# An interaction tower on one core: products read from PSUM instead of from copies, new orders and banks, earlier ids, layer-1 weights in five pieces

## The chip, the cores and the metric

One core of a Trainium2 chip runs the whole kernel. The metric is device time in microseconds of one execution. TensorE (PE in the rows) multiplies matrices, VectorE (DVE), ScalarE (ACT) and GpSimd (POOL) work on elements, SyncE (SP) issues transfers. Matmuls write only PSUM, which has eight banks of 512 fp32 columns on 128 partitions.

## The reference, cut to what matters

```python
e = jnp.stack([tbl_f[ids[:, f]] for f in range(40)], axis=1)   # 512 x 40 x 32
vi, vj = e[:, I, :], e[:, J, :]                                # the 780 pairs i < j
z = jnp.einsum('bke,kef,bkf->bk', vi, W, vj)                   # 512 x 780
h = jnp.concatenate([z, dense_ctx], axis=1)                    # 512 x 796
h = jnp.maximum(h @ W_top1 + b_top1, 0.0)                      # 512
h = jnp.maximum(h @ W_top2 + b_top2, 0.0)                      # 256
y = h @ W_top3
```

## The kernel before, in words

**Quads.** The 40 fields are packed four by four into 10 quads; `emb[:, q, :]` holds quad q as 4 x 32 partitions by 512 batch columns. Quads 0, 1, 3 and 5 are "hot" (tables of 1000 or 1250 rows) and are looked up on TensorE: `spread` (L541) copies the ids to all partitions, ScalarE turns them to fp16 (`ids_to_16`), VectorE (26 of them, L480) or ScalarE (10 of them, two passes, L399 and L402) makes a one-hot tile for each 128 table rows, and `look_up` (L554) multiplies it with the table, split into three bf16 pieces (`rest_of_first`, `third_piece` on VectorE). Quads 2, 4, 6, 7, 8 and 9 are gathered: GpSimd issues 96 indirect DMAs (L375), 16 for each quad in this order, each of 128 rows; `turn` (L572) waits for a quad's 16 and transposes it. ScalarE copies ("lands", L409 and L412) each quad from PSUM into `emb`.

**Pairs.** Group g is one of the 55 pairs (slots quad, stream quad). `map_group` (L584) multiplies the stream quad by the packed pair weights; this fills two operations' worth of PSUM (one where both quads are the same), each a pair of banks, 128 x 1024. There are 100 operations o = 0 to 99. A weight step (`multiply`, L311) multiplies an operation's two banks by `emb` of the slots quad into `prod`, a ring of 8. `sum_ops(b)` (L600) adds over the 32 dimensions of operations 2b and 2b+1 on TensorE into `z_ps`; ScalarE saves it to `zt` after each 8 sums. `layer1` (L617) is the first layer in three parts of z tiles (0, 1), (2, 3), (4), four column blocks m each, and a tail (5, 6). The tail, the second layer (L659) and the output (L665) end the program.

**Who multiplies.** VectorE does 93 operations: 73 read `ring_ps` in PSUM, 20 (COPIED_OPS) read a copy in SBUF, `copied`, that ScalarE makes (L423). GpSimd cannot read PSUM; it does 7 (POOL_OPS) from such copies, behind its 96 gathers.

**Orders and banks.** Each engine's order is written out by hand as a string of letters, and each engine runs it strictly in order. TensorE: i spread, l look-up tile, t turn, m map, s sum, 1 layer 1. VectorE: r pieces, o one-hot, w weight, a layer-1 add. ScalarE: I ids, o one-hot, L land, c copy, z save, 1 layer-1 save. `BANKS` gives the PSUM banks of each step, and `banks_free` (L525) makes TensorE wait until the last user of a bank is done: the weight step of the operation, or only its copy where there is one. Below, M22 is the map of group 22, s16 the sum of operations 32 and 33, w32 the weight step of operation 32, c71 the copy of operation 71, H2.3 tile 3 of hot quad number 2, T6 the turn of quad 6, L1.0 layer 1 of part 1 and block 0.

**Transfers.** ScalarE's queue issues the ids of the hot fields and then those of the gather (`idx`). SP issues tables and pair weights from the start, and the weights of both layers (1792 and 512 KB, L363 and L364) once all look-ups are done; every layer-1 step waits for both.

Of the kernel before, what the change touches and what calls it, by code (L numbers as in the profile page):

```python
# [26 lines left out]
P = 128  # L27
BATCH = 512
CHUNKS = BATCH // P
FIELDS = 40  # L30
DIM = 32
SLOTS = P // DIM
# [18 lines left out]
def quads():  # L51
# [3 lines left out]
    for vocab in HOT_VOCABS:  # L55
# [35 lines left out]
RING_TABLE = 3  # L91
RING_HOT = 2
RING_COPY = 4

PARTS = [(0, 1), (2, 3), (4,)]
TAIL = (5, 6)

TENSOR_ORDER = ("iillllllilllilllllmllmmtlllmlsllslmlllmmssmsmmstslmlllmlslmlllmmlsmssmssmstmsmsmm1mssmssm1mstmmsmssm"  # L100
                "1msmsm1mstmsmmssmssm1mssm1mssm1mtmmssmssm1mssmssms1m11msssmm1s")


BANKS = ("0240624304042065202024024024660240240240240206420242064024026403042402460242026406204024020640241422"
         "4642604204246024024604320402462301")

VECTOR_ORDER = ("rooooorooooooooooroowwwwooowworwwwwwwwwwooowwwowowwwwwwwwwwwwwwwwwwwwwwwwwwwwwwwwwwwwwwwwwwwwwwwwwww"
                "wwwawwwwaawwwwwawwwwwwwaawawwwa")


SCALAR_ORDER = ("IIoIIIIILIoLoLooLooLooozLcccLzc1cLcc1zc1c1ccLcczcccccLcccczcccczc")

POOL_OPS = [77, 78, 80, 85, 87, 93, 98]
COPIED_OPS = [28, 32, 34, 37, 45, 47, 48, 54, 56, 60, 62, 64, 67, 69, 73, 75, 81, 84, 89, 92]
SCALAR_ONE_HOTS = [4, 17, 21, 23, 25, 27, 30, 31, 34, 35]


def z_place(t):
# [64 lines left out]
def build(nc, ctx_rows, ids, hot_ids, tables, hot_tables, w_pairs, consts, vocab_rows, w1, w2, out):  # L183
    with ExitStack() as ctx:
# [6 lines left out]
        def sem(name):  # L191
            return ctx.enter_context(nc.semaphore(name))
# [42 lines left out]
        vocab_loaded = sem("vocab_loaded")  # L235
        const_loaded = sem("const_loaded")
        ctx_loaded = sem("ctx_loaded")
        mlp_loaded = sem("mlp_loaded")
        wload = [sem(f"wload{q}") for q in range(QUADS)]
        gathered = [sem(f"gathered{k}") for k in range(len(GATHERED_AT))]  # L240
        hot_ids_loaded = sem("hot_ids_loaded")
# [95 lines left out]
        @block.sync  # L337
        def _(sp):
            def load_table(h):
                if h >= RING_TABLE:  # L340
                    sp.wait_ge(one_hot_used, FIRST_ONE_HOT[h - RING_TABLE + 1])
                sp.dma_start(table[:, h % RING_TABLE, :width(h)], hot_tables[h]).then_inc(table_loaded[h], 16)

            def load_weights(q):
                first = GROUPS.index((0, q))
                sp.dma_start(wall[:, first:first + q + 1, :].rearrange("p g n -> p (g n)"),
                             w_pairs[:, first * P:(first + q + 1) * P]).then_inc(wload[q], 16)

            load_table(0)
            sp.dma_start(vocab[:], vocab_rows).then_inc(vocab_loaded, 16)  # L350
            load_table(1)
            load_weights(0)
            load_weights(1)
            sp.dma_start(consts_sb[:], consts).then_inc(const_loaded, 16)
            load_weights(2)
            load_table(2)
            for q in range(3, QUADS):
                load_weights(q)
            for h in range(RING_TABLE, len(HOT_AT)):
                load_table(h)  # L360
            sp.dma_start(ctx_sb[:], ctx_rows).then_inc(ctx_loaded, 16)
            sp.wait_ge(one_hot_used, FIRST_ONE_HOT[-1])
            sp.dma_start(w1_sb[:], w1.rearrange("k p n -> p k n")).then_inc(mlp_loaded, 16)  # L363
            sp.dma_start(w2_sb[:], w2.rearrange("(k p) n -> p k n", p=P)).then_inc(mlp_loaded, 16)  # L364
            sp.wait_ge(y_saved, 1)
            sp.dma_start(out.rearrange("(c b) o -> c (b o)", b=P), y_sb[::DIM, :]).then_inc(stored, 16)
            sp.wait_ge(stored, 16)
# [16 lines left out]
        def _(act):  # L384
# [49 lines left out]
                                     bias=b1_sb[:, m:m + 1]).then_inc(lin_saved, 1)  # L434

            act.dma_start(ids_sb[:], hot_ids).then_inc(hot_ids_loaded, 16)  # L436
            act.dma_start(idx[:].rearrange("p c f -> p (c f)"), ids).then_inc(ids_loaded, 16)
            act.wait_ge(hot_ids_loaded, 16)
            nc.scalar.activation(ids_rows[:], ids_sb[:], ACT.Copy).then_inc(ids_rows_done, 1)  # L439
            for kind, what in ACT_STEPS:  # L440
# [83 lines left out]
        def _(pe):  # L524
# [100 lines left out]
            for kind, what in PE_STEPS:  # L625
                if kind == "spread":
                    spread(what)
                elif kind == "hot":
                    look_up(*what)
                elif kind == "turn":  # L630
                    turn(what)
                elif kind == "map":
                    map_group(what)
                elif kind == "sum":
                    sum_ops(what)
                else:
                    part, m = what
                    pe.wait_ge(z_saved, PARTS[part][-1] + 1)
                    pe.wait_ge(mlp_loaded, 32)
                    banks_free(("layer1", what))  # L640
                    layer1(bank(("layer1", what)), PARTS[part], m).then_inc(lin_done, 1)

            pe.wait_ge(z_saved, TAIL[0] + 1)
            for m in range(M1):
                banks_free(("tail", m))
                layer1(bank(("tail", m)), TAIL[:1], m, stop=False)
                if m == 0:
                    sum_ops(LAST // 2)
# [4 lines left out]
            for m in range(M2):  # L653
                for k in range(M1):
                    if m == 0:
                        pe.wait_ge(h1_ready, k + 1)
                    for c in range(COLUMNS):
                        first = m * P + DIM * c
                        mm = nc.tensor.matmul(h2_ps[m][DIM * c:DIM * (c + 1), :], w2_sb[:, k, first:first + DIM],  # L659
# [90 lines left out]
```

## Time and profile before

| | us |
|---|---|
| median of 3 runs | 190.03 |
| lowest and highest | 189.29, 190.49 |
| the profiled execution | 191.81 |
| its span, first to last instruction | 190.0 |

The page gives busy time of each engine. TensorE is busy for 92% of the span, VectorE 78%, GpSimd 61%, ScalarE 48%. "PE L595" and the like in a row name engine and line of the kernel; "idle before" is time in which the engine sat still ahead of an instruction, with what ended it. A matmul in fp32 has two records, so a map of a full group is a row of x16, a sum or one layer-1 step over one z tile x8.

### The profile page before, as it was taken

Reading aid. Unit: us, or ns where it says so; the run is one execution under the profiler, and the core shown is the slowest. Engines: PE = TensorE matmul, PEld = TensorE weight load, DVE = VectorE, ACT = ScalarE, POOL = GpSimd, SP = SyncE. Lnnn points to the kernel's source line nnn. Section 1 sums busy time; section 2 is a strip of 40 time slices with the busy share of each in tenths; the row PEclk is TensorE's granted clock in tenths of the full one; section 3 lists DMA queues with packets and bytes.
Section 4 is the critical chain, followed back from the end, with each engine's and each line's share of the span. In section 5 each row is a group of like instructions: output and inputs, shape, how many; then the busy total and the mean of one; then the engine's idle time right before and its main releaser. Section 6 shows DMA issues by size and latency. Waiting matters only on the chain.

```text
span 190.0 us, 4602 instructions
## 1 busy us (share of the span) xinstructions
PE 174.8 (92%) x1976; PEld 47.3 (25%) x1976; DVE 148.2 (78%) x141; ACT 92.0 (48%) x83; POOL 115.8 (61%) x107
## 2 busy tenths in 40 slices
PE   1999949998999996999999999999999799999993
PEld 0243303321233222122122112222222122222331
DVE  0999987999999786598899898897975868882500
ACT  4877995989699520261072335252255332230421
POOL 0777777877877777778777777877068180522000
PEclk9999999999999999699999999999999999999999
DMA  5999310100000194000111000000000000000000
GB/s 187 388 410 337 106 17 10 19 10 17 16 14 16 39 352 147 17 10 10 17 14 17 11 14 16 13 14 14 3 3 0 0 3 3 0 0 3 0 3 0
DMA packets 7164, 10.80 MB, mean 57 GB/s; under 512 B 2004, under 2 KB 4696, under 8 KB 7144
## 3 DMA queue, kind: packets, MB, share of 16 engines
q1 hardware_dynamic: 3896, 8.81, 12.6%
q0 software_dynamic: 3072, 1.58, 4.8%
q8 instruction: 16, 0.26, 0.6%
q10 hardware_dynamic: 176, 0.12, 0.3%
q14 instruction: 4, 0.03, 0.0%
HBM read 10.50 MB, written 0.00 MB: 55 GB/s over the span
## 4 chain that ended last, share of the span: by engine, by line
PE 55%; POOL 26%; issue 8%; DMA 6%; DVE 2%; ACT 2%; ACTq 0%; DVEq 0%
POOL rows L375 26%; PE ring_ps L595 21%; PE z_ps L612 16%; PE ring_ps L621 13%; PE ring_ps L659 4%; DMA rows<-table,idx 4%; DMA idx<-ids 2%; DVE prod L314 2%; ACT copied L423 1%; PE ring_ps L580 1%; ACT h L458 0%; ACT emb L412 0%; PE ring_ps L665 0%; ACTq L436 0%; DVE y_sb L521 0%
## 5 line engine op out<-in xcount | busy, mean ns | idle before, releaser
L375 POOL DMA_INDIRECT rows<-table,idx x96 | 99.0, 1031 | 33.7 <-issue 28.9
L314 DVE TENSOR_TENSOR prod<-ring_ps,emb 128x1024 f32<-128x1024 f32 x73 | 86.8, 1220 | 16.4 <-PE ring_ps L595 15.6
L595 PE MATMUL ring_ps<-emb,wall 32*64 32x512 f32 (+1 forms) x800 | 61.2, 620 | 3.6 <-DVE prod L314 2.3
L423 ACT ACTIVATE copied<-ring_ps 128x1024 f32<-128x1024 f32 x27 | 27.6, 1025 | 57.7 <-PE ring_ps L595 54.8
L612 PE MATMUL z_ps<-prod,consts_sb 128*32 128x512 f32 x400 | 50.7, 609 | 0.1
L314 DVE TENSOR_TENSOR prod<-copied,emb 128x1024 f32<-128x1024 f32 x20 | 26.6, 1333 | 5.0 <-ACT copied L423 5.0
L314 POOL TENSOR_TENSOR prod<-copied,emb 128x1024 f32<-128x1024 f32 x7 | 16.6, 2377 | 22.5 <-ACT copied L423 22.5
L621 PE MATMUL ring_ps<-zt,w_sb 128*32 128x512 f32 x224 | 26.7, 597 | 0.0
L595 PEld LDWEIGHTS ring_ps<-emb,wall 32*64 32x64 f32 (+1 forms) x800 | 12.9, 131 | 44.3 <-issue 21.1
L399 ACT ACTIVATE distance<-ids,vocab 128x2048 f16<-128x2048 f16 x10 | 20.0, 2000 | 1.7 <-PE ring_ps L567 1.2
L402 ACT ACTIVATE one_hot<-distance,vocab 128x2048 bf16<-128x2048 f16 x10 | 20.0, 2002 | 0.3
L612 PEld LDWEIGHTS z_ps<-prod,consts_sb 128*32 128x32 f32 x400 | 9.9, 109 | 34.9 <-issue 20.6
L480 DVE TENSOR_SCALAR one_hot<-ids,vocab 128x2048 bf16<-128x2048 f16 x26 | 17.9, 746 | 0.4 <-ACT ids L387 0.4
L567 PE MATMUL ring_ps<-one_hot,table 128*32 128x512 bf16 x144 | 14.9, 402 | 0.0
L567 PE MATMUL ring_ps<-one_hot,rest 128*32 128x512 bf16 x144 | 14.6, 394 | 0.0
L567 PE MATMUL ring_ps<-one_hot,third 128*32 128x512 bf16 x144 | 14.6, 393 | 0.0
L621 PEld LDWEIGHTS ring_ps<-zt,w_sb 128*32 128x32 f32 x224 | 6.6, 109 | 18.5 <-issue 16.1
L549 PE MATMUL ring_ps<-ids_rows 16*128 16x512 f16 x16 | 5.8, 500 | 4.5 <-ACT ids_rows L439 4.3
L387 ACT ACTIVATE ids<-ring_ps 128x1024 f16<-128x1024 f32 x8 | 7.8, 1019 | 3.4 <-PE ring_ps L549 3.4
L466 DVE TENSOR_TENSOR rest<-table 128x1024 f32<-128x1024 f32 (+1 forms) x4 | 5.4, 1348 | 4.5 <-DMA table<-hot_table 4.5
L580 PE MATMUL ring_ps<-consts_sb,rows 128*128 128x128 f32 x24 | 3.8, 283 | 4.0 <-DMA rows<-table,idx 3.9
L427 ACT ACTIVATE zt<-z_ps 128x512 f32<-128x512 f32 x6 | 3.6, 595 | 7.5 <-PE z_ps L612 7.5
(25 smaller groups left out, 56.4 us busy)
## 6 DMA issues: line engine op xcount, KB each, us to landing
w_sb<-w SPq DMA_DIRECT2D x1, 1792.0 KB, 8.0
rows<-table,idx POOLq DMA_INDIRECT x96, 2.4
table<-hot_table SPq DMA_DIRECT2D x2, 640.0 KB, 5.5
table<-hot_table SPq DMA_DIRECT2D x2, 512.0 KB, 4.1
wall<-w_pairs SPq DMA_DIRECT2D x1, 640.0 KB
wall<-w_pairs SPq DMA_DIRECT2D x1, 576.0 KB, 9.1
wall<-w_pairs SPq DMA_DIRECT2D x1, 512.0 KB, 8.1
w_sb<-w SPq DMA_DIRECT2D x1, 512.0 KB, 9.8
```

Source lines behind the costliest of these rows:

```text
L314: return eng.tensor_tensor(prod[:, o % RING_P], products, emb[:, slots:slots + 1, :].to_broadcast([P, 2, BATCH]), ALU.mult)
L375: nc.gpsimd.indirect_dma_start(rows[:, k, c, r, :], None, tables[f], bass.IndirectOffsetOnAxis(ap=idx[:, c, f:f + 1], axis=0)).then_inc(ga ...
L387: nc.scalar.activation(ids16[:, h, 2 * half:2 * half + 2, :], pair(("spread", h), half), ACT.Copy).then_inc(ids16_done, 1)
L399: nc.scalar.activation(distance[:], ids16[:, h].rearrange("p r b -> p (r b)"), ACT.Abs, bias=vocab_column(h, t, -1)).then_inc(distance_don ...
L402: nc.scalar.activation(one_hot[:, n % RING_ONE_HOT, :], distance[:], ACT.Relu, bias=vocab[:, 4 * MAX_TILES:], scale=-1.0).then_inc(one_hot ...
L423: nc.scalar.activation(copied_op(o), op_banks(o), ACT.Copy).then_inc(copied_ready, 1)
L480: nc.vector.tensor_scalar(one_hot[:, n % RING_ONE_HOT, :], ids16[:, h].rearrange("p r b -> p (r b)"), vocab_column(h, t), None, ALU.is_equ ...
L567: mm = nc.tensor.matmul(bank(("hot", (h, 0)))[DIM * r:DIM * (r + 1), :], shaped[:, r, t, :], one_hot[:, n % RING_ONE_HOT, r * BATCH:(r + 1 ...
L595: mm = nc.tensor.matmul(pair(("map", g), i // 2)[half, i % 2, :], wall[own, g, half], emb[own, stream, :], start=True, stop=True)
L612: mm = nc.tensor.matmul(z_ps[DIM * g:DIM * (g + 1), :], sel[:, m, :], prod[:, t // 2 % RING_P, t % 2, :], start=m == 0, stop=last)
L621: mm = nc.tensor.matmul(bank[DIM * c:DIM * (c + 1), :], w1_sb[:, k, first:first + DIM], zt[:, k, :], start=start and k == ks[0], stop=stop ...
L659: mm = nc.tensor.matmul(h2_ps[m][DIM * c:DIM * (c + 1), :], w2_sb[:, k, first:first + DIM], h1[:, k, :], start=k == 0, stop=k == M1 - 1)
```

## The change

VectorE takes no operation from a copy any more: COPIED_OPS is empty, so 92 weight steps of VectorE read PSUM, and ScalarE copies only for GpSimd, which has 8 operations (71, 79, 83, 84, 86, 87, 90, 92) in place of 7 (77, 78, 80, 85, 87, 93, 98). The strings of all three orders and of the banks are new. The gather's ids are issued by SP ahead of everything else, in place of second on ScalarE's queue. The layer-1 weights come in four pieces, one for each part, and the second layer's as a fifth; SP issues them after the last look-up and after the third gathered quad has come (`gathered[2]`, quad 6), and each layer-1 part waits for its own piece only.

```diff
--- before.py
+++ after.py
@@ -91,28 +91,29 @@
 RING_TABLE = 3
 RING_HOT = 2
 RING_COPY = 4
+W1_BEHIND = 2
 
 PARTS = [(0, 1), (2, 3), (4,)]
 TAIL = (5, 6)
 
 
 
-TENSOR_ORDER = ("iillllllilllilllllmllmmtlllmlsllslmlllmmssmsmmstslmlllmlslmlllmmlsmssmssmstmsmsmm1mssmssm1mstmmsmssm"
-                "1msmsm1mstmsmmssmssm1mssm1mssm1mtmmssmssm1mssmssms1m11msssmm1s")
-
-
-BANKS = ("0240624304042065202024024024660240240240240206420242064024026403042402460242026406204024020640241422"
-         "4642604204246024024604320402462301")
-
-VECTOR_ORDER = ("rooooorooooooooooroowwwwooowworwwwwwwwwwooowwwowowwwwwwwwwwwwwwwwwwwwwwwwwwwwwwwwwwwwwwwwwwwwwwwwwww"
-                "wwwawwwwaawwwwwawwwwwwwaawawwwa")
-
-
-SCALAR_ORDER = ("IIoIIIIILIoLoLooLooLooozLcccLzc1cLcc1zc1c1ccLcczcccccLcccczcccczc")
-
-POOL_OPS = [77, 78, 80, 85, 87, 93, 98]
-COPIED_OPS = [28, 32, 34, 37, 45, 47, 48, 54, 56, 60, 62, 64, 67, 69, 73, 75, 81, 84, 89, 92]
-SCALAR_ONE_HOTS = [4, 17, 21, 23, 25, 27, 30, 31, 34, 35]
+TENSOR_ORDER = ("iiillllllllillllmlllltlmllmlmllmllslsmlsmsmtllllmsmlmslmlsmslmmllsmsmsmssmstmssmm1mssm1mssmtsmmssmsm"
+                "1msm1mssmssmtmsmssm1mssmtsm1mssm1mmsmssm1msm1sms1m1sm1smssmsms")
+
+
+BANKS = ("0240246025064520520520520464204204204204204204260420462042604205420420462042604204260420462042124602"
+         "4062404204620406246046246024026450")
+
+VECTOR_ORDER = ("oorooooooroooooorooooowowwwowwwoworwwwowowowwwwwwwwwwwwwwwwwwwwwwwwwwwwwwwwwwwwwwwwwwwwwwwwwwwwwwwww"
+                "awwwawwwwwawwwwawaawawwawwwwww")
+
+
+SCALAR_ORDER = ("IIIIoIIoLILLIoooLoLoooozLLz1L11z1LzcLccczccccz")
+
+POOL_OPS = [71, 79, 83, 84, 86, 87, 90, 92]
+COPIED_OPS = []
+SCALAR_ONE_HOTS = [5, 11, 22, 23, 27, 31, 32, 33, 34, 35]
 
 
 def z_place(t):
@@ -235,7 +236,8 @@
         vocab_loaded = sem("vocab_loaded")
         const_loaded = sem("const_loaded")
         ctx_loaded = sem("ctx_loaded")
-        mlp_loaded = sem("mlp_loaded")
+        w1_loaded = [sem(f"w1_loaded{part}") for part in range(len(PARTS) + 1)]
+        w2_loaded = sem("w2_loaded")
         wload = [sem(f"wload{q}") for q in range(QUADS)]
         gathered = [sem(f"gathered{k}") for k in range(len(GATHERED_AT))]
         hot_ids_loaded = sem("hot_ids_loaded")
@@ -346,6 +348,7 @@
                 sp.dma_start(wall[:, first:first + q + 1, :].rearrange("p g n -> p (g n)"),
                              w_pairs[:, first * P:(first + q + 1) * P]).then_inc(wload[q], 16)
 
+            sp.dma_start(idx[:].rearrange("p c f -> p (c f)"), ids).then_inc(ids_loaded, 16)
             load_table(0)
             sp.dma_start(vocab[:], vocab_rows).then_inc(vocab_loaded, 16)
             load_table(1)
@@ -360,8 +363,11 @@
                 load_table(h)
             sp.dma_start(ctx_sb[:], ctx_rows).then_inc(ctx_loaded, 16)
             sp.wait_ge(one_hot_used, FIRST_ONE_HOT[-1])
-            sp.dma_start(w1_sb[:], w1.rearrange("k p n -> p k n")).then_inc(mlp_loaded, 16)
-            sp.dma_start(w2_sb[:], w2.rearrange("(k p) n -> p k n", p=P)).then_inc(mlp_loaded, 16)
+            sp.wait_ge(gathered[W1_BEHIND], 16 * SLOTS * CHUNKS)
+            for part, ks in enumerate([*PARTS, TAIL]):
+                own = slice(ks[0], ks[-1] + 1)
+                sp.dma_start(w1_sb[:, own, :], w1[own].rearrange("k p n -> p k n")).then_inc(w1_loaded[part], 16)
+            sp.dma_start(w2_sb[:], w2.rearrange("(k p) n -> p k n", p=P)).then_inc(w2_loaded, 16)
             sp.wait_ge(y_saved, 1)
             sp.dma_start(out.rearrange("(c b) o -> c (b o)", b=P), y_sb[::DIM, :]).then_inc(stored, 16)
             sp.wait_ge(stored, 16)
@@ -434,7 +440,6 @@
                                      bias=b1_sb[:, m:m + 1]).then_inc(lin_saved, 1)
 
             act.dma_start(ids_sb[:], hot_ids).then_inc(hot_ids_loaded, 16)
-            act.dma_start(idx[:].rearrange("p c f -> p (c f)"), ids).then_inc(ids_loaded, 16)
             act.wait_ge(hot_ids_loaded, 16)
             nc.scalar.activation(ids_rows[:], ids_sb[:], ACT.Copy).then_inc(ids_rows_done, 1)
             for kind, what in ACT_STEPS:
@@ -636,11 +641,12 @@
                 else:
                     part, m = what
                     pe.wait_ge(z_saved, PARTS[part][-1] + 1)
-                    pe.wait_ge(mlp_loaded, 32)
+                    pe.wait_ge(w1_loaded[part], 16)
                     banks_free(("layer1", what))
                     layer1(bank(("layer1", what)), PARTS[part], m).then_inc(lin_done, 1)
 
             pe.wait_ge(z_saved, TAIL[0] + 1)
+            pe.wait_ge(w1_loaded[len(PARTS)], 16)
             for m in range(M1):
                 banks_free(("tail", m))
                 layer1(bank(("tail", m)), TAIL[:1], m, stop=False)
@@ -654,6 +660,8 @@
                 for k in range(M1):
                     if m == 0:
                         pe.wait_ge(h1_ready, k + 1)
+                    if m == 0 and k == 0:
+                        pe.wait_ge(w2_loaded, 16)
                     for c in range(COLUMNS):
                         first = m * P + DIM * c
                         mm = nc.tensor.matmul(h2_ps[m][DIM * c:DIM * (c + 1), :], w2_sb[:, k, first:first + DIM],
```

Written out, TensorE's new order around the turns is:

```
... M0 H1.4 H1.5 H1.6 H1.7 T2 H2.0 M1 H2.1 H2.2 M2 H2.3 M3 H2.4 H2.5 M4 H2.6 H2.7 s0 H2.8 s1 M5
H2.9 s2 M6 s3 M7 T4 H3.0 H3.1 H3.2 H3.3 M8 s4 M9 H3.4 M10 s5 H3.5 M11 H3.6 s6 M12 s7 H3.7 M13 M14
H3.8 H3.9 s8 M15 s9 M16 s10 M17 s11 s12 M18 s13 T6 M19 s14 s15 M20 M21 L0.0 M22 s16 s17 M23 L0.1
M24 s18 s19 M25 T7 s20 M26 M27 s21 s22 M28 s23 M29 L0.2 M30 s24 M31 L0.3 M32 s25 s26 M33 s27 s28
M34 T8 M35 s29 M36 s30 s31 M37 L1.0 M38 s32 s33 M39 T9 s34 M40 L1.1 M41 s35 s36 M42 L1.2 M43 M44
s37 M45 s38 s39 M46 L1.3 M47 s40 M48 L2.0 s41 M49 s42 L2.1 M50 L2.2 s43 M51 L2.3 s44 M52 s45 s46
M53 s47 M54 s48, then the tail, with s49 after its first step
```

and before the change:

```
... M0 H1.6 H1.7 M1 M2 T2 H2.0 H2.1 H2.2 M3 H2.3 s0 H2.4 H2.5 s1 H2.6 M4 H2.7 H2.8 H2.9 M5 M6 s2 s3
M7 s4 M8 M9 s5 T4 s6 H3.0 M10 H3.1 H3.2 H3.3 M11 H3.4 s7 H3.5 M12 H3.6 H3.7 H3.8 M13 M14 H3.9 s8
M15 s9 s10 M16 s11 s12 M17 s13 T6 M18 s14 M19 s15 M20 M21 L0.0 M22 s16 s17 M23 s18 s19 M24 L0.1 M25
s20 T7 M26 M27 s21 M28 s22 s23 M29 L0.2 M30 s24 M31 s25 M32 L0.3 M33 s26 T8 M34 s27 M35 M36 s28 s29
M37 s30 s31 M38 L1.0 M39 s32 s33 M40 L1.1 M41 s34 s35 M42 L1.2 M43 T9 M44 M45 s36 s37 M46 s38 s39
M47 L1.3 M48 s40 s41 M49 s42 s43 M50 s44 L2.0 M51 L2.1 L2.2 M52 s45 s46 s47 M53 M54 L2.3 s48, tail
```

## Rows read from the trace of the kernel before

**Rows 1.** The page, section 1: busy time, share of the span, instructions.

```profile
PE 174.8 (92%) x1976; PEld 47.3 (25%) x1976; DVE 148.2 (78%) x141; ACT 92.0 (48%) x83; POOL 115.8 (61%) x107
```

**Rows 2.** Chain that ended last, in order of time: start us, us, what.

```profile
1.18 3.72 DMA idx<-ids
...
68.22 6.73 DMA rows<-table,idx
```

**Rows 3.** TensorE's timeline: start us, us, line, operation, [idle before <-releaser].

```profile
28.96 0.63 PE L580 MATMUL ring_ps<-consts_sb,rows 128*128 128x128 f32 x4 [2.12 <-DMA rows<-table,idx]
...
46.74 2.14 PE L595 MATMUL ring_ps<-emb,wall 32*64 32x512 f32 x24 [0.52 <-DVE prod L314]
...
49.92 0.63 PE L580 MATMUL ring_ps<-consts_sb,rows 128*128 128x128 f32 x4
...
75.09 0.63 PE L580 MATMUL ring_ps<-consts_sb,rows 128*128 128x128 f32 x4 [1.79 <-DMA rows<-table,idx]
...
88.11 1.11 PE L595 MATMUL ring_ps<-emb,wall 32*64 32x512 f32 x16
89.16 1.92 PE L612 MATMUL z_ps<-prod,consts_sb 128*32 128x512 f32 x16
91.01 1.11 PE L595 MATMUL ring_ps<-emb,wall 32*64 32x512 f32 x16
...
106.59 1.06 PE L612 MATMUL z_ps<-prod,consts_sb 128*32 128x512 f32 x8
108.02 1.12 PE L595 MATMUL ring_ps<-emb,wall 32*64 32x512 f32 x16 [0.37 <-DVE prod L314]
...
140.40 0.66 PE L580 MATMUL ring_ps<-consts_sb,rows 128*128 128x128 f32 x4
...
149.11 1.12 PE L595 MATMUL ring_ps<-emb,wall 32*64 32x512 f32 x16 [1.06 <-DVE prod L314]
...
171.25 1.04 PE L621 MATMUL ring_ps<-zt,w_sb 128*32 128x512 f32 x8
172.39 1.06 PE L612 MATMUL z_ps<-prod,consts_sb 128*32 128x512 f32 x8
```

**Rows 4.** A stretch of 4 us: busy of the engines, granted clock, DMA share, GB/s.

```profile
76.00:80.00 4.00, 4.00 (x40) 0.53 (x24) 2.37 (x2) 1.02 (x1) 3.09 (x4) 0.57 0.10 20
```

**Rows 5.** GpSimd's timeline: gathers and, at the end, products.

```profile
47.36 0.94 POOL L375 DMA_INDIRECT rows<-table,idx  x1 [0.30 <-issue]
...
79.46 1.09 POOL L375 DMA_INDIRECT rows<-table,idx  x1 [0.30 <-issue]
...
125.04 1.85 POOL L375 DMA_INDIRECT rows<-table,idx  x1 [0.30 <-issue]
...
132.19 0.94 POOL L375 DMA_INDIRECT rows<-table,idx  x1 [0.30 <-issue]
...
144.48 2.37 POOL L314 TENSOR_TENSOR prod<-copied,emb 128x1024 f32<-128x1024 f32 x1 [0.43 <-ACT copied L423]
```

**Rows 6.** VectorE's timeline.

```profile
124.85 1.22 DVE L314 TENSOR_TENSOR prod<-copied,emb 128x1024 f32<-128x1024 f32 x1
...
144.54 3.38 DVE L314 TENSOR_TENSOR prod<-copied,emb 128x1024 f32<-128x1024 f32 x1 [2.61 <-ACT copied L423]
```

**Rows 7.** SP's queue: its first DMA issue.

```profile
0.74 0.40 SPq L342 DMA_DIRECT2D table<-hot_table  x1
```

**Rows 8.** DMA issues: operation, count, KB each, us from issue to landing.

```profile
rows<-table,idx POOLq DMA_INDIRECT x96, 2.4
idx<-ids ACTq DMA_DIRECT2D x1, 80.0 KB, 3.7
ids_sb<-hot_ids ACTq DMA_DIRECT2D x1, 33.0 KB, 2.8
```

**Rows 9.** The page, groups: line engine op xcount | busy, mean ns | idle before.

```profile
L423 ACT ACTIVATE copied<-ring_ps 128x1024 f32<-128x1024 f32 x27 | 27.6, 1025 | 57.7 <-PE ring_ps L595 54.8
...
L402 ACT ACTIVATE one_hot<-distance,vocab 128x2048 bf16<-128x2048 f16 x10 | 20.0, 2002 | 0.3
```

## Prediction

> **What bounds the kernel now.** I read the page first: TensorE is busy for 174.8 of 190.0 us, no other engine for more than 148.2 [rows 1]. Its work is the same after the change (the letters of its order are the same, counted), so the time can move only by what TensorE waits, by its clock, and by how its steps are cut. The chain in order of time says who makes it wait [rows 2]: the ids of the gather, then gather after gather on GpSimd until one that is issued at 68.22 lands 6.73 us later, and from 75.09 on TensorE itself, with short stops. The timeline of TensorE gives the stops [rows 3]: 2.12 before T2 at 28.96, 0.52 at 46.74, nothing before T4 at 49.92, 1.79 before T6 at 75.09, about 0.4 before each of two maps (the one at 108.02 is shown), 1.06 at 149.11, and 0.28 before the last sum at 172.39 (a layer-1 step of 0.86 began at 171.25). After T6 the granted clock averages 0.57 over 4 us, between its levels of 2.4 and 1.2 GHz [rows 4]: 4 x 0.43 = 1.7 us lost. After the last sum come 17.6 us of tail, which the change leaves alone.
>
> The unit prices [rows 3]: a full map 1.04 (88.11 to 89.16), a sum 0.93 (two take 1.85, to 91.01), a layer-1 step of two z tiles 1.85, a turn 0.6.
>
> **The ids.** They are issued at 1.18, second on ScalarE's queue, and land 3.72 later [rows 2]. SP issues its first transfer at 0.74 [rows 7]; the ids take that place, 0.44 earlier, and nothing of 512 KB is ahead of them. Bounds for their flight are 2.8 (33 KB issued first on its queue) and 3.7 us [rows 8]; I take 3.0, since they are now first but larger. Landing at 3.75 in place of 4.90: 1.1 us earlier, bounds 0.4 and 1.4. Every gather moves by it. The price is one issue of 0.4 us on SP ahead of its tables and weights; the first table is wanted later than before (VectorE makes two one-hot tiles first), so it costs nothing.
>
> **The start, up to T4.** T2 now stands before M1 and M2, two maps, and TensorE reaches it before its 16 gathers are in, as before [rows 3]: it starts at 28.96 - 1.1 = 27.9, after some 3 us of waiting. From T2 to T4 before, 21.0 us hold ten look-up tiles, seven maps and six sums, with 0.5 of waiting (at 46.74). After, the same stretch holds ten tiles, seven maps and four sums: 21.0 - 1.9 - 0.5 = 18.6. To this I add 1.0 (M1 needs the last ids copy, which ScalarE makes behind the landing of quad 2) and 0.7 (M7 needs the weight step of operation 9, which VectorE makes behind the pieces of hot quad 3): 48.2. ScalarE's one-hot tiles for H2.6 and H2.7 cost two passes of 2.0 each [rows 9] and are ready at about 27.9 + 0.6 + 1.0 + 8.0 = 37.5, just in time. The 32nd gather started at 47.36 and lands 2.4 later [rows 5, 8]; T4 began right then, and moves with it: 49.92 - 1.1 = 48.8. So the gather still decides, with 0.6 us to spare. But less is done by T4: M8, M9, s4 and s5 are still to come.
>
> **T4 to T6.** Before: from 49.92 to 73.3 (75.09 less its wait), 23.4 us without a stop. After: M8, M9 and M18 more (3.1) and s4, s5 more (1.9): 28.4. Here the missing copies cost. Three pairs of banks are in flight, and a map needs two; without a copy the bank comes free only with the product. Where one sum alone lies between two full maps, the rows show what that gives: the sum at 106.59 and the next map at 108.02, 1.43 apart where a sum takes 1.0 [rows 3], so 0.43 each. M16 and M17 are such places: 0.9. T6 is reached at 48.8 + 28.4 + 0.9 = 78.1. Its 48th gather starts 1.1 earlier than 68.22 and lands by 70, since the layer weights, in whose traffic it took 6.73, wait for it. The wait of 1.79 and the slow clock of 1.7 are gone. The first piece of weights (512 KB) is issued at about 70 and wanted at 83.6 by L0.0, 13 us later, so its wait on SP costs nothing. At equal work I am even with before at this point: 78.1 against 75.09 + 1.7 + 1.04 (M18) = 77.8.
>
> **T6 to the last sum.** Before: 172.39 - 75.09 = 97.3. Take away what doesn't come back: 1.7 (clock), 0.43 and 0.41 (the two maps), 1.06 and 0.28, and M18, 1.04. That leaves 92.4. The 1.06 is a clash: VectorE's product from a copy at 144.54 took 3.38 us where others took 1.22, under GpSimd's product from 144.48 to 146.85 [rows 5, 6], and the map at 149.11 waited for VectorE. With no copy read by VectorE it can't recur. The 0.28 I put down to GpSimd's product of operation 98, which the last sum needs; now GpSimd ends with 92. Added: two single-sum places (M29, M31), 0.9; 0.35 where M48 needs the copy of operation 86, which ScalarE (1.03 a copy [rows 9]) makes behind two copies and a z save; and 0.3 for two more changes between maps and sums. Sum: 92.4 + 0.9 + 0.35 + 0.3 = 93.9; the last sum starts at 78.1 + 93.9 = 172.0, 0.4 earlier than 172.39.
>
> VectorE itself: 92 products from PSUM at 1.22 replace 73 at 1.22 and 20 at about 1.23, one product less; GpSimd has the one more, 2.4 us behind its gathers. ScalarE loses 19 copies of 1.03, 19.5 us of work off the path.
>
> **T9, where it decides.** T9 moves ahead of four maps, two sums and two layer-1 steps: 9.7 us. TensorE reaches it at 78.1 + (140.40 - 75.09 - 2.5 - 1.04 - 9.7 + 0.9) = 131.0. The last gather started at 132.19 and would land at 134.6, or 133.5 with the earlier ids. It comes in time only if the gathers also run faster. They do, by these rows: a gather takes 0.94, but ten of those from 79.46 to 125.04 take 0.99 to 1.85, together 4.0 us over [rows 5], and each of the ten runs into a product that VectorE takes from a copy: that at 124.85 ends at 126.07, the gather begun at 125.04 at 126.89 [rows 5, 6]. Gathers beside products from PSUM keep 0.94. So the last one lands at 133.5 - 4.0 = 129.5, 1.5 before TensorE wants it, and the gain of the four us goes into that early T9, not into the end. GpSimd's first product (71, 2.4 us from about 132) is wanted by s35 at about 137.
>
> The Trainium skill ("SBUF — State Buffer", Who interferes with whom) says otherwise of these: a `tensor_tensor` with both inputs in SBUF should block GpSimd's reads but not the writing of descriptors, which the page marks as inferred. By that the gathers would not speed up, and T9 would wait; the trace, with its 1.85 beside 0.94, does not agree. The clash at 144.54 fits its rule on reads.
>
> **Rivals.** *The gathers keep their pace* (slower): the ten long gathers have another cause. T9 then waits 133.5 - 131.0 = 2.5, and with a slow clock after it, as after T6, 4.2: 192.0 to 193.7. It decides once the last gather lands after 131.0. Against it: all ten fit. *The start falls behind*: after about 3 us of waiting before T2 the clock drops, as it did after 1.79 before T6 (but not after 2.12 before the old T2), 1.7 us, of which 0.6 is covered; or ScalarE's tiles come late. T4 is then limited by TensorE: 190.5 to 191.2. *Faster than I think*: ids a further 0.3 earlier, gathers at the start less disturbed, four single-sum places without their 0.43: up to 2.4 less, 187.1. *The change does nothing*: the early work left undone at T4 just pays for the wait at T6; that is in my sum, and nearly so.
>
> **How the numbers follow.** The sum stands against a span of 190.0; that execution took 191.8, and the median of the runs shown is 190.03; I take the difference off the median: 190.03 - 0.4 = 189.6. Chances: my sum, 188.4 to 190.4, 0.5; start behind 0.15; gathers keep their pace 0.1; faster than my sum 0.25. Range 187.3 to 191.8, which leaves out the slow rival and the far end of the fast one. About 1% is what a measurement here can tell from no change: faster by over 1% (under 188.1) 0.26, within 0.60, slower 0.14.
>
> **What would show it.** Right: first gather 1.1 us earlier; no gather over 1.0 us after the last look-up; no wait before T6 and clock 1.00 there; T9 with less than 0.5 of waiting; single-sum maps 0.4 late; no product of VectorE above 1.3. Wrong: a wait before T9, a granted clock under 1 between 25 and 35 us, T4 later than 49.3, or waits of maps on VectorE at more places than the four named, above all where M10 to M13 follow one another, where I found 0.1 to 0.3 us of slack.

## The result, and the profile after

| | median us | runs | span of the profiled execution |
|---|---|---|---|
| before, with the prediction's three runs | 189.33 | 5 | 190.0 |
| after | 191.16 | 5 | 189.7 |

The ratio of after to before is 1.0072, with a 95% interval of 1.0046 to 1.0099: the change costs 0.7%, about 1.4 us. Ratios leave out runs that took over 1.5% more than the fastest of their kernel, medians keep them. I had said 189.6, a gain of 0.4. Every execution of either kernel takes 1.8 to 1.9 us more than its span, so the two columns contradict each other: the profiled spans fall by 0.3 and the medians rise by 1.8. (Part of the 1.8 is the small number of runs: the medians of before in the experiments below are 189.9 to 190.4.) That is the puzzle of this case.

The profile after is close to the one I worked out. TensorE's timeline of the kernel after (start us, us, line, operation, [idle before <-releaser]):

```profile
10.53 0.62 PE L572 MATMUL ring_ps<-one_hot,table 128*32 128x512 bf16 x4 [0.74 <-DVE third L476]
...
16.47 0.39 PE L572 MATMUL ring_ps<-one_hot,third 128*32 128x512 bf16 x4
...
27.44 0.63 PE L585 MATMUL ring_ps<-consts_sb,rows 128*128 128x128 f32 x4 [0.38 <-DMA rows<-table,idx]
...
29.76 1.12 PE L600 MATMUL ring_ps<-emb,wall 32*64 32x512 f32 x16 [0.93 <-ACT ids L393]
...
48.21 0.63 PE L585 MATMUL ring_ps<-consts_sb,rows 128*128 128x128 f32 x4
...
70.67 1.12 PE L600 MATMUL ring_ps<-emb,wall 32*64 32x512 f32 x16 [0.60 <-DVE prod L316]
71.72 1.07 PE L617 MATMUL z_ps<-prod,consts_sb 128*32 128x512 f32 x8
73.28 1.12 PE L600 MATMUL ring_ps<-emb,wall 32*64 32x512 f32 x16 [0.50 <-DVE prod L316]
...
78.22 0.66 PE L585 MATMUL ring_ps<-consts_sb,rows 128*128 128x128 f32 x4
...
131.22 0.66 PE L585 MATMUL ring_ps<-consts_sb,rows 128*128 128x128 f32 x4
...
172.13 1.06 PE L617 MATMUL z_ps<-prod,consts_sb 128*32 128x512 f32 x8
```

T4 is at 48.21 (I had 48.8), with the granted clock at 1.00 from 28 to 36 us, T6 at 78.22 (78.1) without a wait, T9 at 131.22 (131.0) without a wait, the last sum at 172.13 (172.0). M16 and M17 stop for 0.60 and 0.50 (0.43 each in my sum). From T4 to T6 it takes 30.0 us where I had 29.3, and T4 is 0.6 early, so two errors cancel at T6. GpSimd's timeline of the kernel after shows the gathers free of long ones after the last look-up, the last of them 6.2 us earlier than before [rows 5]:

```profile
124.75 0.94 POOL L381 DMA_INDIRECT rows<-table,idx  x1 [0.30 <-PE z_ps L617]
126.00 0.94 POOL L381 DMA_INDIRECT rows<-table,idx  x1 [0.30 <-issue]
```

### The profile page after: what moved, and what is told of

Read it like the earlier page. It is cut to its first block, busy times and chain, and to the rows that moved or that the text cites. A ratio compares the mean times of both kernels' runs of the same rounds, so it can differ in the third digit from the quotient of the medians.

```text
span 189.7 us, 4568 instructions
## 1 busy us (share of the span) xinstructions
PE 176.3 (93%) x1976; PEld 46.3 (24%) x1976; DVE 145.0 (76%) x140; ACT 72.8 (38%) x64; POOL 113.7 (60%) x108
## 4 chain that ended last, share of the span: by engine, by line
PE 70%; POOL 9%; ACT 7%; DVE 5%; issue 5%; DMA 3%; DVEq 0%; ACTq 0%
PE ring_ps L600 26%; PE z_ps L617 20%; PE ring_ps L626 13%; POOL rows L381 9%; PE ring_ps L572 5%; PE ring_ps L667 4%; DVE prod L316 3%; ACT one_hot L408 2%; ACT distance L405 2%; PE ring_ps L585 2%; DMA rows<-table,idx 1%; DMA idx<-ids 1%; DVE one_hot L485 1%; DVE rest L471 1%; ACT copied L429 1%
## 5 line engine op out<-in xcount | busy, mean ns | idle before, releaser
L316 DVE TENSOR_TENSOR prod<-ring_ps,emb 128x1024 f32<-128x1024 f32 x92 | 108.6, 1219 | 20.0 <-PE ring_ps L600 18.6
L381 POOL DMA_INDIRECT rows<-table,idx x96 | 94.7, 987 | 31.8 <-issue 28.6
L316 POOL TENSOR_TENSOR prod<-copied,emb 128x1024 f32<-128x1024 f32 x8 | 18.8, 2372 | 18.0 <-ACT copied L429 18.0
L485 DVE TENSOR_SCALAR one_hot<-ids,vocab 128x2048 bf16<-128x2048 f16 x26 | 18.9, 766 | 7.7 <-ACT ids L393 6.7
L429 ACT ACTIVATE copied<-ring_ps 128x1024 f32<-128x1024 f32 x8 | 8.1, 1024 | 26.8 <-PE ring_ps L600 26.8
L572 PE MATMUL ring_ps<-one_hot,rest 128*32 128x512 bf16 x144 | 15.2, 413 | 0.0
L418 ACT ACTIVATE emb<-ring_ps 128x512 f32<-128x512 f32 x6 | 3.6, 598 | 28.8 <-PE ring_ps L585 28.8
L554 PE MATMUL ring_ps<-ids_rows 16*128 16x512 f16 x16 | 6.7, 559 | 4.2 <-ACT ids_rows L444 3.5
L433 ACT ACTIVATE zt<-z_ps 128x512 f32<-128x512 f32 x6 | 3.6, 593 | 15.3 <-PE z_ps L617 15.3
L439 ACT ACTIVATE h<-ring_ps,consts_sb 128x512 f32<-128x512 f32 x4 | 2.7, 686 | 17.0 <-PE ring_ps L626 17.0
L504 DVE TENSOR_TENSOR h<-ring_ps,h 128x512 f32<-128x512 f32 x8 | 5.5, 683 | 3.0 <-PE ring_ps L626 3.0
```

Source lines behind the costliest of these rows:

```text
L316: return eng.tensor_tensor(prod[:, o % RING_P], products, emb[:, slots:slots + 1, :].to_broadcast([P, 2, BATCH]), ALU.mult)
L381: nc.gpsimd.indirect_dma_start(rows[:, k, c, r, :], None, tables[f], bass.IndirectOffsetOnAxis(ap=idx[:, c, f:f + 1], axis=0)).then_inc(ga ...
L429: nc.scalar.activation(copied_op(o), op_banks(o), ACT.Copy).then_inc(copied_ready, 1)
L485: nc.vector.tensor_scalar(one_hot[:, n % RING_ONE_HOT, :], ids16[:, h].rearrange("p r b -> p (r b)"), vocab_column(h, t), None, ALU.is_equ ...
L572: mm = nc.tensor.matmul(bank(("hot", (h, 0)))[DIM * r:DIM * (r + 1), :], shaped[:, r, t, :], one_hot[:, n % RING_ONE_HOT, r * BATCH:(r + 1 ...
```

## The experiments

Twelve runs, two of them of unchanged kernels, each beside the kernel before on the same chip; "ratio" is to that, with its 95% interval. "Theory A" and so on are those of the quoted expectations.

### Was the profile of before a usual one?

**again**: the kernel before, unchanged.

> The kernel before, unchanged, profiled once more. Theory A (the profiled execution of before was a slow one of its kind: its stop before T6 and the 1.7 us of slow clock behind it are not there, or are shorter, in most executions): the median stays at that of before, and the new profile has a span of 187.3 to 188.5, a granted clock of 1.00 at 76 to 80 us and less than 1.8 us of waiting before T6. Theory B (every execution has that stop, and the time outside the span differs between the two kernels instead): the span is 190 again, with clock 0.57 at 76 to 80 us.

Measured: 190.08 median of 12, against 189.92 of 23 runs of before; ratio 1.0009 (0.9981 to 1.0037). Its profiled execution has a span of 188.4, not 190.0. The 4 us behind T6, in the view of stretches (busy of PE, PEld, DVE, ACT, POOL, then the granted clock), and TensorE's timeline:

```profile
76.00:80.00 4.00, 3.69 (x48) 0.76 (x48) 3.97 (x4) 2.62 (x4) 3.39 (x3) 1.00 0.11 16
```

```profile
29.09 0.63 PE L580 MATMUL ring_ps<-consts_sb,rows 128*128 128x128 f32 x4 [2.26 <-DMA rows<-table,idx]
...
73.83 0.63 PE L580 MATMUL ring_ps<-consts_sb,rows 128*128 128x128 f32 x4 [0.44 <-DMA rows<-table,idx]
...
93.51 0.65 PE L580 MATMUL ring_ps<-consts_sb,rows 128*128 128x128 f32 x4
...
113.82 0.63 PE L580 MATMUL ring_ps<-consts_sb,rows 128*128 128x128 f32 x4 [0.76 <-DMA rows<-table,idx]
...
170.75 1.06 PE L612 MATMUL z_ps<-prod,consts_sb 128*32 128x512 f32 x8
```

The clock is 1.00 where it was 0.57 [rows 4], the wait before T6 is 0.44 where it was 1.79 [rows 3], the last sum starts at 170.75, 1.6 earlier. That is less than the 3.05 of stop and clock that are missing, for two reasons. The first profile's T7 is this one:

```profile
95.95 0.65 PE L580 MATMUL ring_ps<-consts_sb,rows 128*128 128x128 f32 x4
```

From T6 to T7 it took 20.86 us at the lower clock and takes 19.68 here, so the drop cost 1.2 there, not 1.7; and T8 now waits 0.76 where it did not wait before. The listed runs say how rare the drop is: the mean granted clock was 0.991 in the profiled execution of before, and in 3 of the 71 runs of before beside these experiments; those took 190.86, 190.97 and 191.32 where the medians are 189.9 to 190.4. Time alone does not single them out: other runs of this kernel with a clock of 0.998 or more took up to 191.64. Theory A holds. Theory B falls: a run's time exceeds its span by 1.8 to 1.9 in each kernel.

### The parts alone, on the kernel before

**ids**: the gather's ids first on SP.

```diff
-            act.dma_start(idx[:]..., ids).then_inc(ids_loaded, 16)
+            sp.dma_start(idx[:]..., ids).then_inc(ids_loaded, 16)
             load_table(0)
```

> The kernel before with the gather's ids issued first on SP instead of second on ScalarE's queue, nothing else. Theory A (the start up to T4 is set by gathers): the first gather starts 1.9 us earlier, as in the profile after, T2 starts up to 2 us earlier, T4 1 to 2 us earlier, and the time falls by 0.8 to 1.8 us unless the stop before T6 gives it back. Rival (from T2 on TensorE and ScalarE's one-hot tiles set the pace, and the layer weights still fall on quad 6's gathers): below 0.5 us.

Measured: 187.98; ratio 0.9908 (0.9882 to 0.9934). 1.9 us faster. Its rows, GpSimd's first gather and TensorE's turns of quads 2, 4 and 6, none with a wait:

```profile
3.36 1.11 POOL L376 DMA_INDIRECT rows<-table,idx  x1 [2.91 <-DMA idx<-ids]
```

```profile
26.86 0.66 PE L580 MATMUL ring_ps<-consts_sb,rows 128*128 128x128 f32 x4
...
48.55 0.66 PE L580 MATMUL ring_ps<-consts_sb,rows 128*128 128x128 f32 x4
...
71.89 0.66 PE L580 MATMUL ring_ps<-consts_sb,rows 128*128 128x128 f32 x4
```

The gathers start 1.8 us earlier than in the profile of before, and in the old orders all of it comes through in the medians: this part of the change is worth more than I gave it (1.1). Two later kernels, ids84 and ids81, start with the same code as this one, and their T6 is later than its 71.89:

```profile
72.72 0.63 PE L580 MATMUL ring_ps<-consts_sb,rows 128*128 128x128 f32 x4
```

```profile
73.08 0.66 PE L580 MATMUL ring_ps<-consts_sb,rows 128*128 128x128 f32 x4
```

So a single profiled execution of this start fixes T6 only to about 1.2 us.

**w1**: the layer weights in five pieces behind quad 6, as the change has it, nothing else.

> The kernel before with the layer weights in five pieces behind the gathers of quad 6, nothing else. Theory A (most executions of before have only a short stop before T6): T6 starts at about 73.3 without a wait, the granted clock is 1.00 there, and the time falls by 0.3 to 1.5 us on the median of before. Theory B (the stop of 1.8 and the slow clock are in every execution): it falls by 3.3 to 3.6 us. Rival (nothing waits for these loads): within 0.3.

Measured: 189.91; ratio 1.0013 (0.9983 to 1.0042). Nothing that the runs can tell, so the rival's number, but not for its reason: T6 does stop waiting, and T8 waits. TensorE's timeline of this kernel:

```profile
73.56 0.66 PE L585 MATMUL ring_ps<-consts_sb,rows 128*128 128x128 f32 x4
...
113.80 0.63 PE L585 MATMUL ring_ps<-consts_sb,rows 128*128 128x128 f32 x4 [0.98 <-DMA rows<-table,idx]
```

In the run called again T8 also starts at 113.82, with 0.76 of waiting. The gathers of quad 8 are the next thing that is late, so what T6 saves (0.27) is given back there.

**nocopy**: no product of VectorE from a copy, orders and banks as they were.

```diff
-COPIED_OPS = [28, 32, 34, 37, 45, 47, 48, 54, 56, 60, 62, 64, 67, 69, 73, 75, 81, 84, 89, 92]
+COPIED_OPS = []
-SCALAR_ORDER = ("...ooozLcccLzc1cLcc1zc1c1ccLcczcccccLcccczcccczc")
+SCALAR_ORDER = ("...ooozLLz1L1z11LzccLcczcczc")
```

> The kernel before with no operation of VectorE read from a copy (COPIED_OPS empty, the 20 letters c gone from ScalarE's order), orders and banks as they were. Theory A (copies free banks early, and GpSimd's gathers lengthen only beside products from copies): each place of one sum between two full maps costs 0.4 more, some 6 to 8 places, less 1.1 for the clash at 144.5 that goes: +1 to +2.5 us on the kernel before; the last gather starts 4 us earlier (about 128.2), no gather above 1.0 us after the last look-up tile. Rival 1 (the page's rule: a product with two SBUF inputs does not hold up the writing of descriptors): the last gather starts at 132.2 again. Rival 2 (the copies never paid): no change or up to 1.1 us faster.

Measured: 205.03; ratio 1.0796 (1.0772 to 1.0821): 15 us slower, where I had 1 to 2.5. GpSimd's last gather and one stop of TensorE:

```profile
128.71 0.95 POOL L375 DMA_INDIRECT rows<-table,idx  x1 [0.30 <-issue]
```

```profile
110.77 1.07 PE L612 MATMUL z_ps<-prod,consts_sb 128*32 128x512 f32 x8
113.48 1.12 PE L595 MATMUL ring_ps<-emb,wall 32*64 32x512 f32 x16 [1.65 <-DVE prod L314]
```

All waits of maps for a product in this kernel (us in total, times, longest), and the same in the kernel before:

```profile
PE ring_ps L595 <- DVE prod L314: 17.6, 19, 1.6
```

```profile
PE ring_ps L595 <- DVE prod L314: 2.3, 4, 1.1
```

Two results. The gathers: from 61 us on none takes more than 0.95, and the last starts 3.5 us earlier than before; the ten long gathers came from the products from copies, and rival 1 falls here. The banks: in the string of before, all but one of the 20 copied operations give their banks to the next full map; without the copy that map waits for the product of the full map before it, and mostly for its second one. The waits of maps for products grow by 15.3 us, about the whole loss; 18 of the 19 are 0.6 to 1.65 long, and a sum alone between two maps no longer sets the price. In the string of after no map takes the banks of the second operation of the map just before it, unless a copy for GpSimd frees them. So the new orders and banks are not an extra of this change: they buy back most of what the missing copies cost. No run has the new orders with the copies kept, so the two are not separated.

### Undoing parts of the kernel after

**after2**: the kernel after, unchanged, beside the next two.

> The kernel after, unchanged, as the measure for the other runs on this chip. Both theories: 0.4 to 1.0% above the kernel before, span 189.2 to 189.7.

Measured: 191.38 of 12 runs; ratio 1.0064 (1.0041 to 1.0087), span 189.6. The loss stands.

**idsback**: the kernel after with the ids second on ScalarE's queue.

> The kernel after with the gather's ids issued second on ScalarE's queue again. Theory C (T2 now stands where gather and TensorE arrive together, so both count): T2 and T4 come 1.5 to 1.9 us later and the time rises by 1.3 to 1.9 us, as much as the ids alone bring to the kernel before; the last gather lands by 131 and T9 waits little. Rival (TensorE sets the pace up to T4): rises by less than 0.6.

Measured: 194.22; ratio 1.0194 (1.0158 to 1.023). That is 2.5 us above after2 by the ratios (2.8 by the medians, on two chips), more than the 1.3 to 1.9 expected. Its timeline and a stretch say why:

```profile
29.04 0.63 PE L585 MATMUL ring_ps<-consts_sb,rows 128*128 128x128 f32 x4 [2.58 <-DMA rows<-table,idx]
```

```profile
32.00:34.00 2.00, 2.00 (x24) 0.30 (x12) 0.53 (x1) 1.97 (x2) 1.50 (x2) 0.50 0.11 16
```

T2 waits 2.58, another 0.93 comes before M1, and behind them the granted clock is 0.50, the lower level. This is the rival I had called "the start falls behind", 4 of its 6 runs with a mean clock of 0.991 or less; the earlier ids keep the kernel after clear of it. The two runs without it took 193.73 and 193.40.

**w1back**: the kernel after with the layer weights in one piece each behind the last look-up.

> The kernel after with the layer weights in one piece each behind the last look-up, as before the change. Theory (T6 stands late enough for quad 6 even under that traffic, L0.0 needs no piece early): within 0.3 us of the kernel after, no wait before T6. Rival (the pieces are what keeps T6 or T7 from waiting): 0.5 to 2 us slower, with a wait before T6 or T7.

Measured: 191.33; ratio 1.0082 (1.0058 to 1.0107), the same as after2. T6 starts at 77.77 without a wait. The five pieces do nothing that can be measured in either kernel. This kernel starts with the same code as the kernel after, and leaves the half rate of the first look-ups (below) at 13.91 in place of 16.47:

```profile
13.91 0.38 PE L567 MATMUL ring_ps<-one_hot,third 128*32 128x512 bf16 x4
```

**p0**: the kernel after with VectorE's pieces of hot quad 0 ahead of its first one-hot tiles.

```diff
-VECTOR_ORDER = ("oorooooooroooo...
+VECTOR_ORDER = ("rooooooooroooo...
```

> The kernel after, with VectorE making the pieces of hot quad 0 ahead of the first two one-hot tiles, as before the change; nothing else. Theory C (the late first look-up and the longer stretch of matmuls at half rate behind it hold the early part up): H0.0 starts at 9.9 in place of 10.5, the matmuls leave half rate before 14, TensorE is at T2 2 us earlier but must wait for the 16th gather there (27.0), so T2 gains 0.4 and the time falls by 0.3 to 0.5. Rival (look-ups lost at half rate are really on the path): falls by 1.5 to 2.5 us.

Measured: 190.51; ratio 1.0018 (0.999 to 1.0045), against 1.0064 for after2: 0.9 faster than the kernel after, on another chip, and the two intervals just overlap; the other kernels with the start of after, w1back and regroup, lie at 1.0082 and 1.0088. More than expected, less than the rival. Its rows of TensorE:

```profile
14.30 0.39 PE L572 MATMUL ring_ps<-one_hot,third 128*32 128x512 bf16 x4
...
47.03 0.63 PE L585 MATMUL ring_ps<-consts_sb,rows 128*128 128x128 f32 x4
```

The first look-up starts at 9.66 in place of 10.53. Half rate ends at 14.30, which is no gain that this edit can claim, since w1back left it at 13.91 without the edit. T4 is 0.7 to 1.2 earlier than in the four executions that start like the kernel after (47.76 to 48.21). I had thought the gathers would hold T2; but the 16th gather too starts at 23.50 in place of 24.20 to 24.62, and the 32nd at 44.56 in place of 45.27 to 45.71. Why the gathers come earlier is not shown; VectorE's work in SBUF falls elsewhere against them, which is a guess.

**p0i31**: p0, and ScalarE's last ids copy ahead of two landings.

```diff
-SCALAR_ORDER = ("IIIIoIIoLILLIooo...
+SCALAR_ORDER = ("IIIIoIIoLIILLooo...
```

> The kernel after with the pieces of hot quad 0 first and with ScalarE's last ids copy ahead of the landings of quads 1 and 2. M1 then doesn't wait for it (0.93 us in the trace after). Theory C (from T2 to T4 TensorE is bound by its own work and these waits): M1 starts 0.9 earlier, T4 0.5 to 1.3 us earlier, the time falls by 0.6 to 1.5 us on the kernel after. Rival (the 32nd gather or ScalarE's one-hot tiles hold T4 at 48): below 0.4.

Measured: 191.15; ratio 1.0057 (1.0027 to 1.0086), no better than the kernel after and 0.6 above p0 by the medians (3 of its 12 runs have a mean clock of 0.991, 1 of p0's). M1 no longer waits, and T4 does:

```profile
47.69 0.63 PE L585 MATMUL ring_ps<-consts_sb,rows 128*128 128x128 f32 x4 [1.40 <-DMA rows<-table,idx]
```

Its 32nd gather starts at 45.14, in p0 at 44.56. The rival holds: at T4 the gathers stand right behind TensorE.

**regroup**: the kernel after with two sums between M15 and M16 and between M16 and M17, one between M17 and M18.

```diff
-TENSOR_ORDER: ...mmllsmsmsmssmst...
+TENSOR_ORDER: ...mmllsmssmssmsmt...
```

> The kernel after with the sums between M15 and the turn of quad 6 grouped as before the change: two sums between M15 and M16 and between M16 and M17, one between M17 and M18. Theory D (without copies a map behind a single sum waits for the product of the map before, 0.4 to 0.6 each): the stops of 0.60 and 0.50 before M16 and M17 go, one of about 0.4 comes before M18, T6 starts 0.5 to 1.0 earlier, the time falls by 0.4 to 1.0. Rival (VectorE is behind there in any case): T6 within 0.2 of 78.2, time within 0.2.

Measured: 191.69; ratio 1.0088 (1.0057 to 1.0118), no gain on after2. T6 is 1.0 earlier, and the gain is gone two steps later:

```profile
76.02 1.12 PE L600 MATMUL ring_ps<-emb,wall 32*64 32x512 f32 x16 [0.51 <-DVE prod L316]
77.07 0.66 PE L585 MATMUL ring_ps<-consts_sb,rows 128*128 128x128 f32 x4
78.64 1.12 PE L600 MATMUL ring_ps<-emb,wall 32*64 32x512 f32 x16 [0.91 <-DVE prod L316]
```

M16 and M17 stop no more; M18 stops for 0.51 and M19 for 0.91. Theory D is right about each place and wrong about the sum of them: moving a sum moves the stop.

### A version that beats both

**ids84** and **ids81**: the kernel before with the ids first and one copied operation read from PSUM, to take away the clash of a product from a copy with GpSimd's.

```diff
-COPIED_OPS = [..., 75, 81, 84, 89, 92]
+COPIED_OPS = [..., 75, 81, 89, 92]      # ids84; in ids81 84 stays and 81 goes
```

> The kernel before with the ids first on SP and with operation 84 read from PSUM by VectorE instead of from a copy, the one product that clashed with GpSimd's. Theory A (the 3.38 us product is a clash with GpSimd's product): no product of VectorE above 1.3 us near 142, the stop of 1.06 before the map of group 47 becomes 0 to 0.6 (its bank now comes free with the product), the time 0.3 to 1.1 us below that of the ids alone (187.98), so 186.9 to 187.7. Rival (the bank that stays occupied costs as much as the clash): within 0.2 of it.

Measured: 193.39; ratio 1.0104 (1.0041 to 1.0166). It is 5.4 above the ids alone by the medians, so neither theory nor rival came. I had taken the wrong operation. VectorE's row is still there, and TensorE's map of group 47 waits for the product of 84, which stands behind it:

```profile
142.09 3.37 DVE L314 TENSOR_TENSOR prod<-copied,emb 128x1024 f32<-128x1024 f32 x1 [2.61 <-ACT copied L424]
```

```profile
149.00 1.45 PE L595 MATMUL ring_ps<-emb,wall 32*64 32x512 f32 x16 [3.40 <-DVE prod L314]
```

After that stop the clock drops here too (1.45 for a map of 1.12); 5 of its 6 runs have a mean clock of 0.991 or less.

> The kernel before with the ids first on SP and operation 81, whose product from a copy took 3.39 us beside GpSimd's product, read from PSUM (in ids84 the wrong operation was taken: the long product is that of 81, and 84's bank cost 3.4 us of waiting). Theory A (the clash is that of 81): no product of VectorE above 1.3 us, the stop of 1.06 before M47 gone, time 0.7 to 1.2 us below the kernel with the ids alone (1.9 below the kernel before), so 2.6 to 3.1 us below the kernel before. Rival (the copy kept a bank free as in ids84): 0.5 us or more slower than the ids alone.

Measured: 187.80; ratio 0.9879 (0.9835 to 0.9923). The clash is gone, and VectorE waits instead for a sum to free its ring slot; the stop is then 0.64 before M46 in place of 1.06 before M47:

```profile
141.26 2.36 DVE L314 TENSOR_TENSOR prod<-ring_ps,emb 128x1024 f32<-128x1024 f32 x2 [2.49 <-PE z_ps L612]
```

```profile
142.63 1.12 PE L595 MATMUL ring_ps<-emb,wall 32*64 32x512 f32 x16 [0.64 <-DVE prod L314]
```

The gain on the kernel before is 2.1 us, less than the 2.6 to 3.1 expected. Its interval overlaps that of the ids alone (0.9882 to 0.9934), on another chip, so only this is shown: both are about 1% faster than before and 1.5 to 1.8% faster than after; whether the read of 81 from PSUM adds anything stays open.

## Why the prediction was right or wrong, point by point

**The sum against the profiled execution** was right to 0.1 us: 172.0 for the last sum, 172.13 measured. That is partly luck: up to T4 the sum was 0.6 too long, from T4 to T6 0.7 too short. Nearly all the signs of being right that I listed came, and none of being wrong. They could not catch the error, since they are all signs of the kernel after, and the error was in the measure of the kernel before. It is luck too that 191.16 lies inside the range that I gave, and inside the 190.5 to 191.2 of the rival *the start falls behind*: I had a gain where there is a loss, and that rival's slow clock behind T2 is not there.

**The step that failed** is the last one, "I take the difference off the median". Inside the difference stood two terms that belong to one execution and not to the kernel: the 1.79 of waiting before T6 and the 1.7 of slow clock behind it, 3.5 together. In the second profile of before they are 0.44 and 0, and the clock cost only 1.2 in the first. The forecast of 172.0 set against that second execution, with its last sum at 170.75, is 1.25 slower, and that is what the runs show. There was a warning, though a weak one: the table had 191.81 for the profiled execution beside runs of 189.29 to 190.49, and I wrote both down and went on. Against a usual execution, T6 before plus M18 is at 73.83 + 1.04 = 74.9, not 77.8, so the kernel after is behind by 3.35 there, not even. From T6 to the last sum it is ahead: 172.13 - 78.22 = 93.9 against 170.75 - 73.83 - 1.04 = 95.9, 2.0. Together 1.35 slower; the medians of again and after2 differ by 1.30, on two chips.

**Where the 3.35 come from.** The kernel with the ids alone is the fairer measure, since the kernel after has the same ids. Its start is in three executions, of ids, ids84 and ids81, with T6 plus M18 at 72.9, 73.8 and 74.1. So up to there the new orders and the missing copies together lose 4.1 to 5.3 us. Against the first of the three the rows account for 5.1: seven more look-up sets of four matmuls at half rate (0.43 apart in place of 0.215: 1.5) and one spread at half rate (0.9), stops of 4.6 (0.74, 0.66, 0.38, 0.93, 0.81, 0.60, 0.50) against 2.7 in ids; the third spread's wait of 0.35; and three more changes between kinds of steps, at most 0.15 each. The half rate in that list is not the orders' alone: it ended at 11.2, 13.0 and 13.8 in the three executions with one start, and at 13.9 to 16.5 in the four with the other. p0 shows 0.7 to 1.2 by experiment; the others are argued from rows, and p0i31 and regroup show that single stops of that list don't come off by themselves.

**The ids** were mis-sized: 1.9 us earlier at the first gather, not 1.1 (nor 1.4, my bound). Being first, 80 KB landed in about 2.2 us, less than the 2.8 of the smaller transfer that I took for the floor. It changed the mechanism at T2, which waited 0.38, not 3 us. At T4 I had the gather decide, with TensorE 0.6 ahead; it was a tie, the 32nd gather starting at 45.71 and taking 2.3 to 2.4 to land, M7 ending at about the same 48.1.

**The copies.** That gathers run at 0.94 without them was right, and so was T9: the last gather lands at 128.3 (126.00 + 2.3), and TensorE came at 131.2. The rule of the Trainium skill ("SBUF — State Buffer", Who interferes with whom), that such a product does not hold up descriptor writing, which the page marks as inferred, does not agree with these traces: in nocopy every long gather after the last look-up is gone. The slower rival built on it did not come. What a copy is worth as a buffer I knew only for a single sum between two maps; nocopy says 15 us for all 20 with the old banks.

**The clash at 144.54** did vanish in the kernel after, and three of the four single-sum stops were there, 0.1 to 0.2 longer than I had them (M16, M17, M29; at M31 the sum before it waited 0.34 for a z save instead).

**The layer weights**: I let their removal from quad 6's way carry the vanished 3.5. Alone they bring nothing that the runs can tell (w1, w1back).

## What to carry to other kernels

Before a sum is made against a profiled execution, its time is held against the median of the runs: where it lies outside them, find the stretch that makes it so, and count neither that stop nor its removal. Even where it does not, a second profile of the same kernel tells which stops belong to the kernel: here executions of the same code reached T6 up to 1.2 us apart. Signs of being right should test the kernel before as well as the one after. A part that pays on its own (the ids, 1%) should be timed alone before it is tied to new orders that lose it again. Where a copy stands between PSUM and a product, it is a buffer first: leaving it out is priced by which map needs its bank next, not by the copy's own time.

## What the runs showed of the hardware

- A product of VectorE with both inputs in SBUF holds up GpSimd's gathers: a gather that starts under one ends 0.81 to 0.83 us after that product, where that is later than its usual 0.94; the longest took 2.00 (ids84). A product with one input from PSUM does not: with all 93 of them from PSUM (nocopy), no gather from 61 us on takes more than 0.95.
- The granted clock fell to 0.50 behind stops of 2.58 (T2 in idsback), 3.40 (ids84), 1.81 (T2 in nocopy) and 1.79 (T6, one execution of before), and stayed at 1.00 behind 2.12 and 2.26 at the T2 of before and again. So the length of the stop alone does not decide here. One drop cost 1.2 to 1.6 us, by the same stretch with and without it (T6 to T7 20.86 and 19.68; T2 to T4 22.24 in idsback and 20.77 in the kernel after, 22.47 in nocopy and 20.96 in before; in ids84 from M47 to the last sum 24.92, in ids 23.28). The rows of nocopy, its T2 and a stretch behind it:

```profile
29.08 0.99 PE L580 MATMUL ring_ps<-consts_sb,rows 128*128 128x128 f32 x4 [1.81 <-DMA rows<-table,idx]
```

```profile
30.00:32.00 2.00, 2.00 (x21) 0.77 (x24) 1.53 (x3) 0.60 (x1) 1.43 (x2) 0.50 0.05 8
```

- At the start the look-up matmuls run at half rate (0.43 us apart in place of 0.215) while the stretches list a granted clock of 1.00. When it ends differs between executions of the same starting code: 10.9 to 12.8 us (before, again, nocopy, w1), 11.2 to 13.8 (ids, ids84, ids81), 13.9 to 16.5 (after, after2, regroup, w1back). It lasts 2.5 to 5.9 us from the first look-up, and the latest first look-up (11.41, idsback) had one of the shortest, 2.9. What decides it stays open.
